# Attention scores of a fused attention and expert kernel: 16 matmuls of 64 rows by 32 columns per tile in place of 8 of 128 by 64

## The reference, cut to what matters

```python
q = split_heads(layernorm(x) @ Wq.T + bq)          # 16 heads, 8 features each
k = split_heads(ctx @ Wk.T + bk)
scores = einsum('bhqd,bhkd->bhqk', q, k) / sqrt(8)
scores = where(pad_mask == 0, -1e9, scores) + src_mask
p = softmax(scores)
x = x + tanh(g0) * ((p @ v) @ Wo.T + bo)
x = x + tanh(g1) * experts(layernorm(x))           # all in float32
```

## Time and profile before

| | us |
|---|---|
| median of 3 runs (lowest to highest) | 1036.06 (1035.89 to 1036.55) |
| span of the profiled execution, first to last instruction | 1026.3 |
| what lies around the span (the difference to the median) | 9.8 |
| TensorE matmuls busy in the span | 720.7 (70%) |
| VectorE busy | 771.3 (75%) |
| ScalarE busy | 569.9 (56%) |
| GpSimd busy | 601.1 (59%) |
| score matmuls (L367), 1024 records, busy | 145.3 |
| mask adds (L535), 128, busy | 86.6 |
| mean granted TensorE clock | 0.881 of 2.4 GHz |

### The profile page before, as it was taken

The page is one execution under the profiler, slowest core; times in us unless marked ns, Lnnn a source line. Parts: engine busy times, 40 slices in busy tenths (PEclk is TensorE's granted clock), DMA queues, the critical chain, the costliest instruction groups (busy, mean ns, idle before and its releaser), DMA issues. The chain is left out here.

```text
span 1026.3 us, 24733 instructions
## 1 busy us (share of the span) xinstructions
PE 720.7 (70%) x6890; PEld 556.4 (54%) x6891; DVE 771.3 (75%) x2206; ACT 569.9 (56%) x1195; POOL 601.1 (59%) x655
## 2 busy tenths in 40 slices
PE   2788778777776877887755798888998898850000
PEld 1455555454454544555435698888888887740000
DVE  5799999899898999999954975444444444436996
ACT  2767666766567666677422245555555554526553
POOL 5444466666666666666537904666666666650544
PEclk9889998989899899899856999999999999985555
DMA  4211111221112212111017201222222221215432
GB/s 119 49 37 47 42 53 44 69 59 49 52 42 68 59 50 71 42 33 33 29 45 227 68 0 53 62 59 62 62 62 62 59 62 57 62 55 149 129 117 82
DMA packets 91309, 66.22 MB, mean 65 GB/s; under 512 B 17008, under 2 KB 80752, under 8 KB 91248
## 3 DMA queue, kind: packets, MB, share of 16 engines
q1 hardware_dynamic: 70048, 35.49, 14.0%
q0 software_dynamic: 8448, 17.45, 5.4%
q10 hardware_dynamic: 12752, 12.58, 3.7%
HBM read 38.21 MB, written 23.09 MB: 60 GB/s over the span
## 5 line engine op out<-in xcount | busy, mean ns | idle before, releaser
L842 POOL TENSOR_TENSOR prob<-prob,mx 128x1024 f32<-128x1024 f32 x64 | 121.6, 1900 | 162.4 <-DVE mx L542 162.4
L1294 POOL DMA_INDIRECT expert_results<-y,dest x136 | 148.4, 1091 | 82.7 <-POOL dest L1290 56.2
L1108 ACT ACTIVATE hT<-bank,b1g_c,gate_c 128x256 f32<-128x256 f32 x272 | 138.3, 558 | 87.5 <-PE bank L76 87.5
L166 POOL DMA_INDIRECT expert_lists<-xn,slots x128 | 125.0, 976 | 56.9 <-issue 30.6
L1049 PE MATMUL bank<-w,hT 128*128 x1088 | 139.6, 281 | 24.1 <-ACT hT L1108 20.4
L367 PE MATMUL bank<-kbd,qg 128*64 128x256 f32 x1024 | 145.3, 427 | 6.1 <-DVE prob L535 4.9
L1049 PEld LDWEIGHTS bank<-w,hT 128*128 128x128 f32 x1088 | 127.2, 191 | 39.2 <-issue 39.2
L775 ACT ACTIVATE PT<-bank 128x512 f32<-128x512 f32 x128 | 69.2, 594 | 62.1 <-PE bank L378 62.0
L367 PEld LDWEIGHTS bank<-kbd,qg 128*64 128x64 f32 x1024 | 74.3, 152 | 52.6 <-issue 22.7
L384 PE MATMUL bank<-w_att,aT 128*128 128x128 f32 x128 | 34.2, 353 | 93.2 <-DVE aT L528 69.8
L535 DVE TENSOR_TENSOR prob<-bank,mask 128x512 f32<-128x512 f32 x128 | 86.6, 677 | 7.4 <-PE bank L367 7.1
(11 more groups left out here) (183 smaller groups left out, 1751.2 us busy)
## 6 DMA issues: line engine op xcount, KB each, us to landing
rows<-expert_lists SPq DMA_DIRECT2D x70, 130.0 KB, 2.2
yin<-expert_results SPq DMA_DIRECT2D x16, 512.0 KB, 5.5
x_all<-in_x SPq DMA_DIRECT2D x16, 256.0 KB, 2.8
ctx_in<-in_ctx SPq DMA_DIRECT2D x16, 256.0 KB, 3.1
pad_k<-in_mask_BxS_ik SPq DMA_DIRECT2D x16, 256.0 KB, 4.0
xn2T<-x2T ACTq DMA_DIRECT2D x16, 256.0 KB, 2.3
out<-res ACTq DMA_DIRECT2D x7, 512.0 KB, 3.2
expert_results<-y,dest POOLq DMA_INDIRECT x136, 2.3
```

The lines of the kernel that those rows point to most:

```text
L166: po.indirect_dma_start(lists[:, :], bass.IndirectOffsetOnAxis(ap=m.slots[:, par, t, k:k + 1], axis=0), m.xn2[:, par, t, :], None).then_in ...
L842: po.tensor_tensor(ps, ps, mx[:, u, :].unsqueeze(2).broadcast_to([P, H, S]), ALU.subtract).then_inc(subbed, 1)
L1108: ac.activation(hT[:, par, c, :], h_ps[par][c // 2][:, (c % 2) * SL:(c % 2 + 1) * SL], ACT.Gelu, bias=b1g_c[:, c, bass.ds(e, 1)], scale=ga ...
L1294: po.indirect_dma_start(results[:, :], bass.IndirectOffsetOnAxis(ap=dest[:, par, h, :], axis=0), y[:, par, h, :], None).then_inc(sent[par] ...
```

## The change

The scores of a tile become 16 matmuls of 64 rows by 32 columns, in one piece. `qg` has two slots in place of four: groups 0 and 2 share slot 0, groups 1 and 3 share slot 1. Of a slot, partitions 0 to 63 hold one group and zeros, partitions 64 to 127 another group and zeros. For each slot s, each half of the rows and each quarter r of the 128 queries, a matmul takes its 64 rows of `qg` and `kbd` and writes 32 partitions of `sc_ps[half]`; a half of the rows holds the groups that went to that bank before. PE waits once a tile for both mask adds of the tile before (with `apart=True`), and a tile's last matmul counts `scores_done` up by 2. Where u is 3, the router's transpose (L396) now stands behind all the scores. POOL's first memset (L824) is half as large.

```diff
-        qg = sb("qg", [P, 2, NG, QW])
+        qg = sb("qg", [P, 2, 2, QW])
...
-            def scores(n, u, par, q, h):
-                if u == 0 and h == 0:
+            def scores(n, u, par, q):
+                if u == 0:
                     need(pe, q_ready, q, per=NG, total=NQ)
                     need(pe, k_ready, q, per=HG, total=NQ)
-                need(pe, masked, n - 1, per=2, k=h + 1)
-                for g in (2 * h, 2 * h + 1):
-                    for b in range(2):
-                        i = pe.matmul(sc_ps[h][b * S:(b + 1) * S, (g % 2) * 256:(g % 2) * 256 + 256],
-                                      qg[:, par, g, u * P + b * S:u * P + (b + 1) * S],
-                                      kbd[:, par, 2 * u + b].rearrange("p j k -> p (j k)"), start=True, stop=True)
-                i.then_inc(scores_done, 1)
+                need(pe, masked, n - 1, per=2, k=2, apart=True)
+                for s in range(2):
+                    for half in range(2):
+                        rows = slice(64 * half, 64 * half + 64)
+                        for r in range(4):
+                            i = pe.matmul(sc_ps[half][32 * r:32 * r + 32, s * 256:s * 256 + 256],
+                                          qg[rows, par, s, u * P + 32 * r:u * P + 32 * r + 32],
+                                          kbd[rows, par, 2 * u + r // 2].rearrange("p j k -> p (j k)"),
+                                          start=True, stop=True)
+                i.then_inc(scores_done, 2)
...
-                        if exists(n, NT):
-                            scores(n, u, par, q, h)
+                        if h == 0 and exists(n, NT):
+                            scores(n, u, par, q)
...
-                            ac.activation(qg[r, 1 - par, g, :], fa_ps[r, :], ACT.Identity, bias=cols[r, 3:4],
+                            ac.activation(qg[r, 1 - par, g % 2, :], fa_ps[r, :], ACT.Identity, bias=cols[r, 3:4],
```

## The result

| | median us (lowest to highest, runs) | ratio to before, 95% interval |
|---|---|---|
| before, beside it | 1035.97 (1031.69 to 1036.55, 4) | |
| the changed kernel | 1048.6 (1044.72 to 1052.78, 4) | 1.0127 [1.0103, 1.0151] |

12.6 us slower: 1035.3 was forecast, and 1048.6 lies above the range of 1029 to 1043. The profiled execution of the changed kernel has a span of 1042.8 us and a time of its own of 1044.72, so 1.9 us lie around its span.

The account below looks back on a forecast made before the run. DVE was taken to bound attention, a faster PE paying only where DVE waits for scores. 1026.3 - 1.8 (half 1's adds) + 0.3 (the joint wait) + 0.7 (clock) = 1025.5 us span, plus 9.8 around it: 1035.3 us, range 1029 to 1043.

Parts of the forecast that it names:

- The sum around the span: Outside the profiled span: 9.8 us (median less span) added to the forecast span of 1025.5, giving 1035.3 us.
- The sum of the span: Whole profiled span: 1026.3 - 1.8 + 0.3 + 0.7 = 1025.5 us.
- Eight side by side: Score matmuls on PE: eight run at once, a tile's 32 records take 1.08 us, 1.95 at the low clock.
- The adds' waits: DVE's mask adds waiting for scores: 7.1 us in 10 waits falls to 5.3 us in about five, half 0's.
- a gain of 1.8: Mask add of half 1: its five waits for scores vanish, -1.8 us.
- DVE as the bound: Attention, 100 to 500 us: DVE sets the pace and stays busy for some 384 us of 400.
- The clock: PE's granted clock, 100 to 500 us: falls from 0.92 to about 0.90 with longer pauses, +0.7 us.
- The third rival: PE's clock in attention: stays low for most tiles, half 0's add waits every quad, 1041 us; chance 0.15.
- The transposes' cover: Router's transpose, moved behind all scores: still ready before DVE reads it, with half a microsecond of cover, 0 us.
- The second rival: Scores on PE: row halves run in turn, 1.95 us a tile, half 0's adds held up, 1052 us; chance 0.12.

Follow-up runs that it names:

- e6: The changed kernel, unchanged, run again beside the kernel before on a chip where counts come on time: 1024.9 us, ratio 1.0001.
- e10: The changed kernel, unchanged, run once more beside the kernel before where counts come on time: ratio 1.001 [0.9993, 1.0027].
- e5: The kernel before, unchanged, profiled again on a chip where counts come on time: 1024.5 us.
- e9: The kernel before, unchanged, repeated in a second set where counts come on time: ratio 0.9996 [0.9981, 1.0011].
- e17: The kernel before, unchanged, one more look; no late counts: 1022.91 us.
- e13: The kernel before, unchanged, repeated in a third set where counts come on time: ratio 1.0005 [0.9989, 1.0021].
- e16: The kernel before, unchanged, one more look; no late counts: 1024.95 us.
- joint: Kernel before with its 8 score matmuls in one piece, one wait, one count by 2, router's transpose behind: 1038.55 us (1.0142); with late counts 1045.97 (1.0115).
- e18: The kernel before, unchanged, run on a chip where counts come late: 1039.51 us, and 1036.19 in the run beside it.
- e1: The changed kernel with two 64-column halves for four quarters, 16 records a tile, where counts come late: 1036.74 us, 1.001 of the kernel before.
- e4: The changed kernel with qg kept at its old four slots and larger memset, where counts come late: 1053.92 us, 1.0137 of the kernel before.

## Why the prediction was wrong, point by point

**The sum around the span: the step that failed.** "With the 9.8 us around it (median less span)" took two executions of different kinds for one, and took the term over to the changed kernel as it was. Only 1.9 us lie around a span (1044.72 less 1042.8, 1023.96 less 1022.0; in no run more than 2.4). The profiled execution of before would thus have taken some 1028.2 us, an estimate, below the lowest of the timed runs (1031.69). The other 8 us were time that the timed runs had and the trace had not. No trace of those runs is on record, but their times are those of the kind with late counts. For the changed kernel the same term came out at 23.1 us (1048.6 less the 1025.5 of span that was forecast): the change made it larger, by late counts of the scores (12.0 us in its trace) that hold up DVE. The front showed the sign, 9.8 us beside a spread of 0.7 over three runs, and the prediction passed over it with a constant. The mechanism that decided stood in none of the cases, and of the named rivals none had its place.

**The sum of the span was right where its trace holds.** Forecast was 0.8 us less than before; measured 1.0001 and 1.001 with intervals of some 0.2%, where no count is late. The single terms:

- Eight side by side: forecast 1.08 us at the high clock and 1.95 at the low, measured 1.09 and 1.96. That the halves of the rows write different banks fits the rule cited from the Trainium skill, "TensorEngine Tiling (Array Packing)", "Gotcha 1: PSUM Pressure"; no run here put both halves in one bank.
- The adds' waits: forecast 5.3 us in about five; measured 4.2 in 7 (e6) and 5.9 in 8 (e10), against 6.1 in 11 (e5) and 8.6 in 13 (e9). The unchanged kernel's traces on time spread from 4.8 us (e17) to 9.5 (e13), so a gain of 1.8 can't be told, neither in the waits nor in the time.
- DVE as the bound: 383.4 of 400 us in e6, 384 forecast. TensorE's 35 us less (273.7 against 309.0) bought nothing.
- The clock fell from 0.92 to 0.87 and not to 0.90, in e6 as in after. The third rival had this mechanism, but at 0.87 it cost no time that can be seen.
- The transposes' cover: 0 us, right where no count is late. The waits for it are 9.1 us in e6 (4.6 of them one wait) and 7.4 in e10, against 7.0 (e5) to 8.5 (e16) in the unchanged kernel.

**The second rival came near to a price, in part by luck, and its condition did not come true.** Each quad was to cost 1.0 us, 16 in all, for the add of half 0 if the scores of a whole tile took 1.95 us. `joint` has just that and costs 13.8 us. But its adds wait only 5.0 us more than in e13_before, 0.3 a quad; the router's copy, which the rival's sum left out, makes up the rest with 4.7. In the change the scores take 1.09 us, and this price isn't paid. What is paid is another: a late count of the scores holds up the add of half 0 and the chain behind it. Whether two counts a tile would have spared the change that isn't shown: `joint`, with one count a tile and 16 records, has no late score count either.

**The drain** (the stretch behind the last tile) was weighed nowhere in the prediction, since the change touches nothing there. It is where the unchanged kernel loses some 8 of the 11 us that separate its two kinds of executions.

## What to carry to other kernels

Before a span is turned into a time, subtract it from the time of its own execution, not from the median; where the rest is more than the 2 us seen here, the trace and the timed runs may not be the same kind of execution, and a sum on the trace says nothing of the difference. A report split in two is a reserve: one wait and one count for a tile, with the router's transpose behind them, cost 13.8 us where the scores stay as slow, and what pays for it must do so in every kind of execution. And where packing an array gives the same duration with half the instructions (two 64-column halves, 1.09 us in 16 records, as against 32), take the fewer: where counts come late, the form with 16 was level with before (1.001) and the form with 32 was not (1.0137).

## What the runs showed of the hardware that was not expected

- A count of TensorE on a semaphore can come long after the records that it reports have ended: 2.3 us behind 32 score records, 6.6 (e18) to 8.7 us (e1) behind 8 logit records. All 223 late ones in attention fell due beside an indirect DMA of GpSimd, yet on another chip the waiting engine starts 0.06 us after the logits at the same place (e6). In the profile such a wait is put down to "remote", or to a matmul that had long ended.
- By chip, the same unchanged kernel takes 1021.0 to 1031.0 us (e5 to e17) or 1033.0 to 1039.6 (beside e1 to e4, and e18), with medians 11 us apart, at about the same granted clock (0.888 in e5_before_again, 0.88 in e18_before).
- Two row halves by four column quarters of the array run at once in float32: 32 records of 256 columns in 1.09 us. 64 rows by 64 columns, 16 records, take the same, so here neither the issue nor the loads of the 32 set the time.
